# A token-routed feed-forward block: results kept in the place of their gathered rows, and second results of mixed tiles put aside in DRAM

## What is computed

```python
x = x + attention(layernorm(x), ctx)      # relu projections, scores, values; relu of each
z = layernorm(x)
logits = z @ gate_w                        # [4096, 8]
topv, topi = top_k(logits, 2);  w = softmax(topv)
u, v = z @ Wu[e], z @ Wv[e];  s = silu(u) * v;  y = s @ Wo[e]
out = x + w[0] * y[topi[0]] + w[1] * y[topi[1]]
```

## Time and profile before

| | us |
|---|---|
| median of 3 runs | 446.25 |
| lowest, highest | 442.06, 461.91 |
| the profiled execution | 438.34 |
| its span, first to last instruction | 436.6 |
| PE, DVE, ACT, POOL busy in it | 405.3, 334.3, 266.5, 220.4 |

### The profile page before, as it was taken

One profiled execution on the slowest core, in us unless ns is written; L12 is line 12 of the kernel. 1 busy time (PEld: TensorE's weight loads), 2 busy tenths in 40 slices (PEclk: granted clock), 3 DMA queues, 4 the chain that ended last, 5 costly groups with the idle time before them and its releaser, 6 DMA issues.

```text
span 436.6 us, 10196 instructions
## 1 busy us (share of the span) xinstructions
PE 405.3 (93%) x3062; PEld 361.0 (83%) x3062; DVE 334.3 (77%) x1107; ACT 266.5 (61%) x581; POOL 220.4 (50%) x231
## 2 busy tenths in 40 slices
PE   8999999999999999989888779989999999999880
PEld 6698988888998888977777668979999999999760
DVE  2779899999999999999645668867887666666541
ACT  1777778777778778868464446656766444444320
POOL 2011245555656665553466443332333588888874
PEclk9999999999999999999999899999999999999996
DMA  8812235767766666535946437869654378999994
GB/s 290 256 59 93 88 112 186 251 240 247 246 219 222 214 238 204 169 121 163 315 169 217 150 121 241 260 216 299 200 185 119 88 139 153 186 175 168 202 182 61
DMA packets 47492, 81.46 MB, mean 187 GB/s; under 512 B 8272, under 2 KB 19024, under 8 KB 47312
## 3 DMA queue, kind: packets, MB, share of 16 engines
q1 hardware_dynamic: 32576, 46.69, 34.5%
q0 software_dynamic: 14864, 34.11, 29.6%
HBM read 42.09 MB, written 46.34 MB: 203 GB/s over the span
## 4 chain that ended last, share of the span: by engine, by line
PE 38%; DVE 31%; issue 8%; SPq 6%; DMA 6%; ACT 5%; another core or an unknown queue 3%; POOL 2%; POOLq 1%; DVEq 0%; ACTq 0%
PE psQ L1424 7%; PE psQ L1422 7%; PE psQ L1423 6%; DVE st L1045 6%; PE psT L1418 5%; DVE x L1034 4%; DVE qpT L866 3%; DVE qT L866 2%; SPq L502 2%; DMA out_dram<-xin,qpT 2%; PE psQ L1418 1%; DVE mv L1049 1%; DVE wuv L866 1%; PE psO L1422 1%
## 5 line engine op out<-in xcount | busy, mean ns | idle before, releaser
L866 DVE TENSOR_TENSOR qT<-psT,qT 128x512 fp32r<-128x512 f32 x103 | 69.4, 687 | 38.1 <-ACT qT L662 30.1
L1422 PE MATMUL psQ<-wuv,qT 128*128 x284 | 86.8, 306 | 0.0
L568 POOL DMA_INDIRECT z_dram<-zb x64 | 70.8, 1106 | 31.2 <-issue 14.9
L1423 PE MATMUL psQ<-wuv,qT 128*128 x284 | 81.0, 285 | 0.0
L1424 PE MATMUL psQ<-wuv,qT 128*128 x284 | 80.7, 284 | 0.0
L1422 PE MATMUL psQ<-qT,wq 128*128 128x256 f32 x256 | 75.1, 293 | 0.0
L662 ACT ACTIVATE qT<-psT 128x512 fp32r<-128x512 f32 x103 | 59.4, 593 | 22.5 <-PE psT L1418 16.2
L1424 PE MATMUL psQ<-qT,wq 128*128 128x256 f32 x256 | 72.4, 283 | 0.0
L1423 PE MATMUL psQ<-qT,wq 128*128 128x256 f32 x256 | 72.4, 283 | 0.0
L1422 PEld LDWEIGHTS psQ<-wuv,qT 128*128 128x128 f32 x284 | 54.2, 191 | 4.2
L730 ACT ACTIVATE gate_work<-psQ 128x128 f32<-128x128 f32 x71 | 19.6, 276 | 59.8 <-PE psQ L1424 48.4
(11 more groups left out here) (313 smaller groups left out, 1078.9 us busy)
## 6 DMA issues: line engine op xcount, KB each, us to landing
wq<-z_dram SPq DMA_DIRECT2D x42, 264.0 KB
xin<-in_x_dram SPq DMA_DIRECT2D x11, 512.0 KB, 3.9
z_dram<-spare SPq DMA_DIRECT2D x17, 264.0 KB, 4.2
qpT<-z_dram SPq DMA_DIRECT2D x17, 264.0 KB
kpT<-z_dram SPq DMA_DIRECT2D x10, 264.0 KB
zT_ctxT<-in_x_dram SPq DMA_DIRECT2D x5, 512.0 KB, 3.6
z_dram<-z_dram SPq DMA_DIRECT2D x8, 264.0 KB
maskT<-in_mask_1xSxS_ff_dram SPq DMA_DIRECT2D x16, 128.0 KB, 4.3
```

The lines of the kernel that those rows point to most:

```text
L568: pool.indirect_dma_start(out=z_dram, out_offset=bass.IndirectOffsetOnAxis(ap=z_of(b)[:, t, ROW_COL + k:ROW_COL + k + 1].bitcast(U32), axi ...
L866: nc.vector.tensor_tensor(o, a, b, ALU.subtract).then_inc(s, 1)
L1422: pe.matmul(o, w[LO], a[HI], start=first, stop=False)
L1423: pe.matmul(o, w[HI], a[LO], start=False, stop=False)
```

## The change

It has three parts.

1. The ring becomes twenty places (two of `xn`, seven of `wq`, three each of `qpT`, `kpT`, `vp`, two of `stage`), and a result lies in the first 512 columns of its tile's place: `res` and `held` are gone, and with them the waits for result buffers. `again` works in place and waits for the tile's transposes.
2. A mixed tile is stored twice at once: its first choices to the output, and its rows of second choices, whole (528 numbers, the token number among them), packed into the DRAM tensor `aside_dram` at rows that DVE computes once (`aside_to`). When tiles 25 to 38 have landed SP reads the 896 rows back in 7 plain loads, and POOL adds them to the output in 7 transfers, after tiles 45, 48, ... 63.
3. In the blocks: the strips of logits are turned by transposes and added by DVE (`folded`), `pick` is gone; ACT normalizes both token tiles of the next x (but for the first block); POOL takes rstd1 before exp of the gap; DVE turns x before it keeps the statistics and makes norm1's shift between the two additions of the attention; PE's scores wait for each chunk's low half alone.

```diff
-RES_B = 9
-RING = 12
+RING = 20
+BACK = HELD // 2
...
+        zg = [xn[:, i, :] for i in range(2)]
+        for flat, n in ((wq_flat, 7), (qpT_flat, 3), (kpT_flat, 3), (vp_flat, 3), (stage, 2)):
+            zg += [flat[:, i * ROW:(i + 1) * ROW] for i in range(n)]
+        back = [zb[:, i, t, :] for i in range(ZBUFS) for t in range(TPB)] + [xin[:, :, :, :].rearrange("p a t d -> p (a t d)")[:, 0:ROW]]
...
         def res_of(t):
-            return res[t % RING] if t < FULL else res[(t - FIRST_B) % RES_B]
-        def held_done(h):
-            return FIRST_B + 4 * h // 3
+            return zg_of(t)[:, 0:D]
+        def landed(t):
+            return 16 * sum(2 if is_held(u) else 1 for u in range(t % RING, t + 1, RING))
+        def back_wanted(k):
+            return FIRST_B + RING + k
+        def back_done(k):
+            return FIRST_B + 6 + 3 * k
...
+                if t == 15:
+                    sp.wait_ge(o_done, 2 * NB)
+                if t == 18:
+                    sp.wait_ge(stage_lo, 3 * E)
                 q = t % RING
-                ge(sp, res_stored[q], 16 * rounds(t))
+                if t >= RING:
+                    sp.wait_ge(res_stored[q], landed(t - RING))
                 sp.dma_start(zg_of(t), z_dram[bass.ds(row_of(t), P)]).then_inc(z_loaded[q], 16)
+            def load_back(k):
+                if k == 0:
+                    for a in range(FULL, FIRST_B):
+                        sp.wait_ge(res_stored[a % RING], landed(a))
+                    sp.wait_ge(x1_ready, 2 * NB)
+                sp.dma_start(back[k], aside_dram[k * P:(k + 1) * P, :]).then_inc(back_loaded[k], 16)
...
-            def store_firsts(t):
+            def store_held(t):
+                h = t - FULL
                 pool.wait_ge(res_ready, t + 1)
                 pool.indirect_dma_start(
-                    out=out_rows, out_offset=bass.IndirectOffsetOnAxis(ap=own_to[:, t - FULL, 1:2], axis=0),
-                    in_=held[t - FULL], in_offset=None, bounds_check=TOK - 1, oob_is_err=False).then_inc(res_stored[t % RING], 16)
-            def store_held(h):
+                    out=out_rows, out_offset=bass.IndirectOffsetOnAxis(ap=own_to[:, h:h + 1], axis=0),
+                    in_=res_of(t), in_offset=None, bounds_check=TOK - 1, oob_is_err=False).then_inc(res_stored[t % RING], 16)
                 pool.indirect_dma_start(
-                    out=out_rows, out_offset=bass.IndirectOffsetOnAxis(ap=own_to[:, h, 0:1], axis=0),
-                    in_=held[h], in_offset=None, bounds_check=TOK - 1, oob_is_err=False,
-                    compute_op=ALU.add).then_inc(held_stored, 16)
+                    out=aside_dram, out_offset=bass.IndirectOffsetOnAxis(ap=aside_to[:, h:h + 1], axis=0),
+                    in_=zg_of(t), in_offset=None, bounds_check=BACK * P - 1, oob_is_err=False).then_inc(res_stored[t % RING], 16)
+            def store_back(k):
+                pool.wait_ge(back_loaded[k], 16)
+                pool.indirect_dma_start(
+                    out=out_rows, out_offset=bass.IndirectOffsetOnAxis(ap=back[k][:, TOK_COL:TOK_COL + 1].bitcast(U32), axis=0),
+                    in_=back[k][:, 0:D], in_offset=None, bounds_check=TOK - 1, oob_is_err=False,
+                    compute_op=ALU.add).then_inc(back_stored, 16)
...
+                if nxt.real:
+                    rstd1_of(nxt)
                 if third.real:
                     exp_gap(third)
-                if nxt.real:
-                    rstd1_of(nxt)
...
-                nc.scalar.activation(res_of(t), zg_of(t)[:, 0:D], ACT.Identity, bias=zg_of(t)[:, MEAN_COL:MEAN_COL + 1],
-                                     scale=zg_of(t)[:, STD_COL:STD_COL + 1]).then_inc(x_again, 1)
+                act.wait_ge(z_loaded[t % RING], 16 * (rounds(t) + 1))
+                act.wait_ge(g_turned, t + 1)
+                nc.scalar.activation(res_of(t), res_of(t), ACT.Identity, bias=mean, scale=std).then_inc(x_again, 1)
...
+                    norm1(nxt, 0)
                     norm1(nxt, 1)
...
+                    nc.vector.tensor_reduce(logits[:, :, :], ps_strips, AX.X, ALU.add).then_inc(folded, 1)
+                    ge(dve, folded, self.b.n + 1)
                     for t in range(TPB):
-                        nc.vector.max(top_v[:, t, :], ps_logit[:, t, :]).then_inc(route, 1)
+                        nc.vector.max(top_v[:, t, :], logits[:, t, :]).then_inc(route, 1)
...
                     add_attention(prv, 0)
-                    add_attention(prv, 1)
                 if nxt.real:
                     norm1.shift()
-                    norm_x(nxt)
+                if prv.real:
+                    add_attention(prv, 1)
...
                     norm2.shift()
-                    keep_stats(prv)
                 for t in range(TPB):
                     if nxt.real:
                         turned_x(nxt, t)
                     else:
                         turned_g(t)
+                if prv.real:
+                    keep_stats(prv)
...
-                ge(pe, qp_lo, 4 * b.n + 4)
                 for c in range(DC):
+                    ge(pe, qp_lo, 4 * b.n + c + 1)
                     ins = three(psS[:, 0:BT], [kpT[:, h, c, g * KEYS:(g + 1) * KEYS] for h in range(2)],
...
                 for t in range(TPB):
-                    ins = pe.matmul(ps_logit[:, t, :], logT[:, t * P:(t + 1) * P], pick[:, :], start=True, stop=True)
+                    ins = turn(ps_log[:, t * P:(t + 1) * P], logT[:, t * P:(t + 1) * P])
...
+                    pe.matmul(ps_sums, ones[:, :], cuts[:, :], start=True, stop=False)
+                    pe.matmul(ps_sums, ones[:, :], sums[:, :], start=False, stop=True)
```

More of the change, by code:

```diff
@@ L69 @@
 CONSTS = 20
-PLANNED = (10, 25, 53)
+PLANNED = (10, 25, 54)
 def ge(eng, sem, value):
@@ L98, in rounds @@
     return t // RING
-def in_slot(q, tiles):
-    return len(range(q, tiles, RING))
 def moe_block(nc, x, ctx_in, mask, kq, kk, kv, bq, bk, bv, gate_w, Wu, Wv, Wo, out):
@@ L125, in moe_block, with early @@
         z_dram = dram("z_dram", [NROWS, ROW])
-        wq = sb("wq", [P, 2, DC, D], F32R)
+        aside_dram = dram("aside_dram", [BACK * P, ROW])
+        with ExitStack() as first_use:
+            def early(name, shape):
+                return first_use.enter_context(nc.sbuf_tensor(name, shape, F32R))
+            wq = early("wq", [P, 2, DC, D])
+            qpT = early("qpT", [P, 2, DC, BT])
+            kpT = early("kpT", [P, 2, DC, NBATCH * KEYS])
+            vp = early("vp", [P, 2, NBATCH, D])
+        wq_flat = sb("wq_flat", [P, 2 * DC * D])
+        qpT_flat = sb("qpT_flat", [P, 2 * DC * BT])
+        kpT_flat = sb("kpT_flat", [P, 2 * DC * NBATCH * KEYS])
+        vp_flat = sb("vp_flat", [P, 2 * NBATCH * D])
         wuv = sb("wuv", [P, E, 2, DC * 2 * R], F32R)
         wo = sb("wo", [P, E, 2, D], F32R)
-        kpT = sb("kpT", [P, 2, DC, NBATCH * KEYS], F32R)
-        vp = sb("vp", [P, 2, NBATCH, D], F32R)
         qT = sb("qT", [P, 2, DC, BT], F32R)
-        qpT = sb("qpT", [P, 2, DC, BT], F32R)
         lgT = sb("lgT", [P, 2, BT], F32R)
@@ L194, in moe_block @@
         logT = sb("logT", [P, BT])
+        logits = sb("logits", [P, TPB, E])
         top_v = sb("top_v", [P, TPB, 8])
@@ L246, in moe_block @@
         away = sb("away", [P, HELD, K])
+        sums = sb("sums", [P, HELD], BF16)
         own = sb("own", [P, HELD, 5])
-        own_to = sb("own_to", [P, HELD, K], U32)
+        own_to = sb("own_to", [P, HELD], U32)
+        aside_to = sb("aside_to", [P, HELD], U32)
         psT = [bank(f"psT{i}") for i in range(2)]
@@ L350, in moe_block @@
         own_ready = sem("own_ready")
-        held_stored = sem("held_stored")
+        back_loaded = [sem(f"back_loaded{i}") for i in range(BACK)]
+        back_stored = sem("back_stored")
         res_stored = [sem(f"res_stored{i}") for i in range(RING)]
@@ L515, in _ @@
                     copy_tail(t - EARLY)
-            for q in range(RING):
-                sp.wait_ge(res_stored[q], 16 * in_slot(q, TILES))
-            sp.wait_ge(held_stored, 16 * HELD)
+                for k in range(BACK):
+                    if back_wanted(k) == t:
+                        load_back(k)
+            for a in range(TILES - RING, TILES):
+                sp.wait_ge(res_stored[a % RING], landed(a))
+            sp.wait_ge(back_stored, 16 * BACK)
         @block.gpsimd
@@ L650, in _ @@
                 if is_held(t):
-                    store_firsts(t)
+                    store_held(t)
                 else:
                     store(t)
-                for h in range(HELD):
-                    if held_done(h) == t:
-                        store_held(h)
+                for k in range(BACK):
+                    if back_done(k) == t:
+                        store_back(k)
         @block.scalar
@@ L988, in lists_cuts @@
                 link(nc.vector.tensor_scalar(cuts[:, :], ident[:, 0:HELD], cut_f[:, 0:1], None, ALU.mult))
```

(1 more changed line is left out.)

72 lines of the change are left out of this document (21 added, 51 removed).

## The result

The kernel after takes 445.82 us (median of 20 runs, 444.12 to 449.08), the kernel before 442.15 us (median of 20): ratio 1.0099, 95% interval 1.0074 to 1.0123. It is one per cent slower. I had predicted 435.5 us, which is 2.4% under the 446.25 us known then and 1.5% under the 442.15 of twenty runs. The profiled execution took 446.55 us, its span 444.7, mean granted clock 0.98. Medians here are of all runs of a kernel, while ratios compare fast runs alone, since some executions are slower for no reason in the kernel; so a ratio isn't always the quotient of the two medians.

A forecast was written before the change was run, and what follows sets the result against it. DVE and PE together were taken to bound the blocks, POOL's 46 adds the end. Gains of 4.5 (end) and 4.9 us (blocks), passage 0, took 438.34 to 428.9; with 6.6 carried over, 435.5 us, range 424 to 446.

The forecast's parts named there:

- part 1: The end: 39 adds instead of 46, POOL no longer the bound, 4.5 us gained; second stores in mixed tiles cost 0.
- wait at tile 39: POOL's wait there, 2.00 us before, covers one store more, +1.3 us, taken back by POOL's new slack.
- within 0.3: Sign for the end: POOL's last add is issued within 0.3 us of the last result.
- Part 2, the blocks: Attention blocks: period falls from 11.85 to 11.50 us, 14 x 0.35 = 4.9 us gained.
- Part 3, the passage: From 195 to 294 us: SyncE's chain is the anchor and stays; sum 0, bounds -2 and +2.
- The sum: 4.5 + 4.9 = 9.4 us off the profiled 438.34, then 6.6 of the median's surplus carried: 435.5 us.
- median's surplus: Median of three other runs lies 7.9 us above the profiled execution; 6.6 carried over, 1.3 taken as gone.
- A: Rival, the end: bound by the DMA engines, so the 4.5 us are given back; 440.0 us, chance 0.15.
- B: Rival, the blocks: they stay at 11.85 us, ACT's bubble and jitter taking the gain; 440.4 us, chance 0.18.
- C: Rival, the blocks: ACT becomes the loop, 12.6 us a block; 451.7 us, slower, chance 0.07.
- D: Rival, the passage: ACT's unexplained stand of 4.74 us before 241.53 goes as well; 430.2 us, chance 0.15.

The follow-up runs named there:

- b2: The kernel before with part 3 of the change alone (the orders of token steps in the attention blocks): 437.97 us, ratio 0.9930.
- c4: The same kernel as b2, unchanged, run again on a chip with the effect: 437.99 us, ratio 0.9918 to the kernel before.
- c1: The kernel after, unchanged, run again on a chip with the effect: 443.85 us, ratio 1.0103 to the kernel before.
- p1: The kernel before with results of tiles 0 to 7 written by SyncE's plain transfers instead of POOL's indirect ones: 437.32 us, ratio 0.9884.
- n1: The kernel after without the 14 second plain stores, the 7 loads back and the 7 adds: 432.63 us against 440.66, ratio 0.9799.
- n2: The kernel after with second results of mixed tiles written whole by 14 plain SyncE transfers, and 46 adds instead of 39: 445.38 us, ratio 1.0119.
- b1: The kernel before with an empty second plain indirect POOL issue behind each of the 14 mixed tiles' stores: 451.57 us, ratio 1.0222.
- b4: b1 with the empty second issue behind every second mixed tile only, 7 of 14: 450.66 us, ratio 1.0168 to the kernel before.
- b3: b1 with the empty second issue of the adding kind instead of the plain one: 450.94 us, ratio 1.0201 to the kernel before.
- b7: The kernel before with two empty plain indirect issues behind the four scatters of each of the first 12 blocks: 461.98 us, ratio 1.0708.
- third set: Four kernels, b6 and b7 among them, run on another chip, where the kernel before takes 430.87 us instead of 440 to 443.
- b6: b1 with the empty issue cut to 32 of 128 partitions, on the third set's chip: 432.39 us, ratio 1.0011 to the kernel before.
- c3: The same kernel as b6, unchanged, run again on a chip with the effect: 454.68 us, ratio 1.0394 to the kernel before.

## Why the prediction was wrong

**The step that failed** is in part 1: "two with their 0.30 are 2.56 to 2.69 us, against the 2.675 of a tile. POOL just keeps up ... I take 0." The durations were right (0.98, 0.30, 0.98) and POOL did keep up. What I had put at nothing without a row for it was what an issue does to the other engines: 0.9 us of the tile loop each, 14 of them, 12.5 us. (Nor does the bound of 14 x 0.13 follow: two stores of 1.11 us, with their 0.30, are 2.82 us, 0.15 over a tile; with 2.69 it is 0.2 us in all.) I had written that I would be wrong outright if mixed tiles took over 2.7 us; they take 3.5. I had bounded that cost from POOL's side only (0 to 2 us late), and no row of the kernel before has two plain stores in close order in the steady tiles. But its passage had them, beside the 4.74 us that I called unexplained. Had I asked what POOL did then, the price could have been bounded: up to 4.7 us for six issues. Why close plain issues do this stays open.

**Part 1, the end.** The bound did move: 39 adds, PE without a break from 360 to 420 us, no wait for a load. From tile 41 to the last result 3.5 us were gained, of which 0.3 are lost behind it. The last add goes out at 436.94, 1.5 us behind its result (434.72 + 0.75), not within 0.3: an adding issue takes 1.86 us with its gap, and the one in front of it was not through. So about 3.2 of the 4.5 us. The wait at tile 39 was 2.65, as predicted longer (2.00 + up to 1.3).

**Part 2, the blocks.** 11.53 us a block against 11.50 predicted. At tile 0 it is worth 3.0 us, not 4.9. The first block's second addition comes 0.6 us later than before (35.02 and 34.43 us), and from there to the last block's 3.6 us are gained: ten of the fifteen periods gain 0.25 to 0.34 us, the others 0.0 to 0.23.

**Part 3, the passage.** I took 0 with bounds of 2, and called SyncE's chain an anchor that would take back what comes before it. In after 3.0 us of gain at tile 0 became 0.2 at tile 10, so it looked right. The other runs show it wasn't: tile 25 starts at 300.9 us in before and 300.0 in after, but at 295.5 in b2, 298.2 in c4 and 296.8 in c1. So the passage hands a gain on, give or take some 3 us of scatter: tiles 0 to 10 took 42.0 us in c1 and 47.3 in after, two executions of one kernel. That late signals make this scatter is my reading; p1 is the one run that bears it out.

**The sum.** n1 is the nearest to the forecast's world, the kernel after without the second issues (and without the seven loads and adds): 8.0 us less than before, where my steps gave 9.4. The median's surplus of 7.9 us, of which I carried 6.6, was a matter of three runs; with 20 it is 3.8. With 3.8 in its place the forecast would have been 432.7 us, so this error hid part of the other. That 445.82 lies inside my range, by 0.2 us, is luck: its upper end stood for A, B and the median's surplus, none of which came, and neither end is the sum of the terms that it names (435.5 - 5.3 - 1.4 is 428.8, not 424; A or B with 2 more and 7.9 for 6.6 is 443 to 444, not 446).

**The rivals.** A (DMA engines full) fell: they were at 0.94 of the time from 360 to 420 us while PE had no wait, and the stretched tiles had a share of 0.63. The Trainium skill, DMA: Bandwidth & Descriptors, section "Issuing engines are not separate DMA queues", says that transfers of all issuers share the same engines; by that the aside traffic would be the suspect, and n2, which moves it from SyncE at 2.7 us a tile with a share of 0.86, shows that it isn't. B and C (blocks) fell with 11.53. D, the stall, had the right object and the wrong sign: it came again at the same place in b1 (5.4 us) and b4 (4.8 us), and by p1 it is most likely the mechanism that the change brought to the mixed tiles as well.

## What to carry to other kernels

Don't count POOL's plain indirect DMA issues as work of POOL alone: here each one added to the mixed tiles, in rows of three or four, cost 0.7 to 1.0 us of a loop of 2.675 us, whatever it moved (though none on one of the chips, and none steadily in the blocks), so a design that saves adding transfers at the end (3.2 us gained here) by more plain ones in the middle of a full loop (12.5 us lost) can lose. When a trace shows a stand with an end that it can't name, look what every other engine was issuing then, before calling it luck. And compare variants on one chip, by the interval of one repeated instruction rather than by the total: n2, b3 and b7 had totals that pointed to the wrong cause.

## What the runs showed of the hardware that I had not expected

TensorE's signals, or its matmuls, come late, by up to 5.4 us going by ACT's stands (b1; DVE's `top_v`, which waits for TensorE as well, stood up to 3.0 us in b4, so it isn't ACT alone), while POOL issues plain indirect DMAs at one per 1.28 us in rows of three or more in the tile phase; with adding ones at one per 1.86 us hardly (0.2 us per issue), and with memsets of the same length not at all. The price is no lower for 32 rows than for 128, and it is there for issues that move nothing. The blocks, with four such issues in a row each, show no steady one (11.86 and 11.87 us on the two kinds of chip). It is there on the chips of three of the four sets and of the main comparison; on the chip of the third set the same kernel (b6 and c3) shows nothing, none of that set's four traces has a single wait with a remote end from 208 us on, while each of the fourteen others has three or more (4.8 us and more in all), tiles 0 to 10 take 35 to 37 us instead of 40 to 48, and the kernel before runs 2 to 3% faster; by b6, whose tile 0 starts when that of before does (212.8 and 212.9 us), all of that comes from the passage. What sets these chips apart, whether matmuls or only their signals are late, whether a lone pair costs anything, and what the kernel after takes on the chip without the effect (it wasn't run there) stay open.
